# Convolution diagonals built on chip, and W1 loads issued two pairs ahead

## The chip, the cores and the metric

One Trainium2 chip, all 8 cores, each with two of the 16 sequences. The time is that of one launch, in device microseconds of the slowest core. TensorE, VectorE, ScalarE and GpSimd compute; SyncE (SP) and GpSimd (POOL) issue the DMAs.

## The reference, cut to what matters

A pre-norm transformer layer on x of [16, 2048, 1024]: attention with 16 heads, then a feed-forward part with quantised weights and activations.

```python
def bit_linear(x, w):   # activations to int8 steps per row, weights to -1, 0, 1
    xq = x + stop_gradient(act_quant(x) - x)
    wq = w + stop_gradient(weight_quant(w) - w)
    return einsum('bsd,hd->bsh', xq, wq)
h = bit_linear(x, w1)                      # 1024 -> 4096
h = depthwise_conv1d(h.transpose(0, 2, 1), conv_w, conv_b)   # 3 taps, each channel by itself
h = silu(h.transpose(0, 2, 1))
return bit_linear(h, w2)                   # 4096 -> 1024
```

## The kernel before

Each core runs the same program. It first prepares the weights: it casts those of the attention, then (tensor `p_dg`) it builds diagonal matrices for the convolution, and then `wprep` quantises and transposes w1 and w2. These go to HBM: `t_w1t` holds, for each of 32 chunks of 128 hidden channels, 8 blocks of 128x128 bf16 of w1 and 3 diagonal blocks, one for each tap; `t_w2t` holds w2. The diagonal of tap j and chunk hc is the identity times `cw_t`, one VectorE operation per block, 96 in all. Three DMAs from GpSimd write them out, and a barrier of all engines ends the stage.

Then each sequence goes through projections, attention and the feed-forward part. The latter works in `NCT` = 4 blocks of 512 positions (`t`, lines 1191 to 1197). `emit_g1_w1_conv(t)` walks over 16 pairs of chunks (`g`, line 1098). For a pair SyncE issues the load of `w1b`: two chunks of 11 blocks, 704 KB in pieces of 256 bytes, into one of two halves of the buffer. Each chunk is multiplied by 16 matmuls of 257 positions (`w1_chunk`) into the PSUM tile `hps`; VectorE scales the result and writes it to `Hbq` as bf16; three matmuls with the diagonals of the chunk, each on `Hbq` moved by one position, make the convolution in the same PSUM bank (`emit_conv_silu`), and ScalarE writes its silu to `Hb2`. The convolution of a chunk is issued behind the matmuls of the next chunk. A chunk's matmuls wait for the silu of the chunk two before, since they write to its bank.

`emit_mx` keeps the running maximum and minimum of `Hb2` on VectorE, a batch of 4 chunks every second pair. Behind the last pair `emit_chain` makes the scales of the second product out of them: a chain of small steps between VectorE and TensorE. With these scales `emit_hq_batch` rounds `Hb2` to `hqg`, 4 chunks a call.

The second product of block t-1 is issued between the chunks of block t: `emit_w2_sub`, twice a pair, 8 matmuls of 512 columns, with a load of 512 KB of `w2b` (two halves of a buffer, `w2b_cons`). Pairs 0 to 7 make the first 256 positions of the block, pairs 8 to 15 the others. Behind pair 7 and pair 15 `emit_final_pair` evicts two 128-row outputs, one after the other, through the single buffer `obuf`, and the next half product waits for `ve_ev`, the last of these evictions. The second product of the last block runs by itself at the end.

The order on each engine is that in which the calls are written. So on SyncE the loads stand in the order w1 of pair g, w2 of its first half product, w2 of its second. The load of w1 waits for all matmuls issued so far:

```python
if t > 0 or g >= 2:
    r.wait(r.sync, tn, tn.v)
dl_w1[g] = dw1[wb].inc(r.sync.dma_start(...))
r.wait(r.tensor, dw1[wb], dl_w1[g])
```

Nearly every instruction is replayed from one line, so the profile shows line 80 for all; tiles tell them apart.

Of the kernel before, what the change touches and what calls it, by code (L numbers as in the profile page):

```python
# [7 lines left out]
F32 = mybir.dt.float32  # L8
BF16 = mybir.dt.bfloat16
# [82 lines left out]
def build_program(nseq, S):  # L92
# [22 lines left out]
    t_tri = nc.dram_tensor("trimask", [128, 128], BF16, kind="ExternalInput").ap()  # L115
    t_o8 = nc.dram_tensor("ones8s", [8, 128, 8], BF16, kind="ExternalInput").ap()
    t_out = nc.dram_tensor("out", [nseq, S, D], F32, kind="ExternalOutput").ap()
    t_w1t = nc.dram_tensor("w1t_s", [32, 11, 128, 128], BF16, kind="Internal").ap()
    t_wq4 = nc.dram_tensor("wq4_s", [4, 128, 8192], BF16, kind="Internal").ap()
    t_w2t = nc.dram_tensor("w2t_s", [32, 128, D], BF16, kind="Internal").ap()  # L120

# [24 lines left out]
    ctrs = {n: Ctr(nc, es, n) for n in  # L146
            ("bar", "dl", "dw", "dst", "tn", "sc", "ve", "gp",
             "dlx0", "dlx1", "dlx2", "dlx3", "dlb0", "dlb1",
             "dw1a", "dw1b", "dw2a", "dw2b")}
    bar, dl, dw, dst = ctrs["bar"], ctrs["dl"], ctrs["dw"], ctrs["dst"]  # L150
    tn, sc, ve, gp = ctrs["tn"], ctrs["sc"], ctrs["ve"], ctrs["gp"]
    dlx = (ctrs["dlx0"], ctrs["dlx1"], ctrs["dlx2"], ctrs["dlx3"])
    dlb = (ctrs["dlb0"], ctrs["dlb1"])
    dw1 = (ctrs["dw1a"], ctrs["dw1b"])
    dw2 = (ctrs["dw2a"], ctrs["dw2b"])

    r = Rec(nc)
# [45 lines left out]
    with nc.sbuf_tensor("p_wst", [128, 4096], F32) as wstg, \  # L203
         nc.sbuf_tensor("p_wbf", [128, 8192], BF16) as wbf:
        ve_cast = [0, 0]
        dw_w = 0
        for i4, t_w in enumerate((t_qw, t_kw, t_vw, t_ow)):
            if i4 < 3:
                wsrc = t_w.rearrange("h (mc p) d -> mc p h d", p=128)
            else:  # L210
                wsrc = t_ow.rearrange("(hp hh) d m -> hp (hh d) m", hh=2)
            for k4 in range(4):
                par = k4 % 2
                if i4 + k4 > 0:
# [25 lines left out]
        r.wait(r.gpsimd, dw, dw.v)  # L240
        r.emit()
        barrier()
        r.emit()

    with nc.sbuf_tensor("p_dg", [128, 32 * 384], BF16) as dstg:
        ve_dg = 0
        for hc in range(32):
            for j in range(3):
                ve_dg = ve.inc(r.vector.tensor_scalar(
                    dstg[:, hc * 384 + j * 128:hc * 384 + (j + 1) * 128],  # L250
                    ident_f32[:, :],
                    cw_t[:, j * 32 + hc:j * 32 + hc + 1], 0.0,
                    ALU.mult, ALU.add))
        r.wait(r.gpsimd, ve, ve_dg)
        for j in range(3):
            dw.inc(r.gpsimd.dma_start(
                out=t_w1t[:, 8 + j].rearrange("hc p f -> p hc f"),
                in_=dstg.rearrange("p (hc j f) -> p hc j f", hc=32, j=3)
                [:, :, j, :]), 16)
        r.wait(r.gpsimd, dw, dw.v)  # L260
        r.emit()
        barrier()
        r.emit()
# [114 lines left out]
    for s in range(nseq):  # L378
# [389 lines left out]
        if True:  # L768
# [14 lines left out]
            for tq in range(NT // 4):  # L783
# [96 lines left out]
            G1sb = es_c.enter_context(  # L880
                nc.sbuf_tensor(f"c_g1b{s}", [128, 514], F32))
            w1b = es_c.enter_context(
                nc.sbuf_tensor(f"c_w1b{s}", [128, 2 * 2816], BF16))
            w2b = es_c.enter_context(
                nc.sbuf_tensor(f"c_w2b{s}", [128, 2 * 2048], BF16))
            ct1 = es_c.enter_context(
                nc.sbuf_tensor(f"c_t1{s}", [128, 2 * 512], F32))
            ct2 = es_c.enter_context(
                nc.sbuf_tensor(f"c_t2{s}", [128, 2 * 512], F32))
# [13 lines left out]
            sc_sil = [0] * 32  # L903
            ve_hq = [0] * 32
            tn_cv = [0] * 32
            ve_mx = 0
            ve_ev = 0
            ve_g1 = 0
# [66 lines left out]

            def emit_conv_silu(t, hc):
                par = hc % 2
                gpair = hc // 2
                dbase = ((gpair % 2) * 2 + (hc % 2)) * 1408 + 1024
                r.wait(r.tensor, ve, ve_h[hc])  # L980
                for j in range(3):
                    tn.inc(r.tensor.matmul(
                        hps[:, par * 1024:par * 1024 + 512],
                        w1b[:, dbase + j * 128:dbase + (j + 1) * 128],
                        Hbq[:, hc * 514 + j:hc * 514 + j + 512],
                        start=(j == 0), stop=(j == 2)))
                tn_cv[hc] = tn.v
# [44 lines left out]
            def emit_g1_w1_conv(t, w2t=None):  # L1032
# [37 lines left out]
                def w1_chunk(hc, wb):  # L1070
# [5 lines left out]
                    lbase = (wb * 2 + (hc % 2)) * 1408  # L1076
                    for fc in range(8):
                        wsl = w1b[:, lbase + fc * 128:lbase + (fc + 1) * 128]
                        tn.inc(r.tensor.matmul(
# [15 lines left out]
                                [[2048, 128], [512, 2], [1, 257]]),  # L1095
                        G1sb.rearrange("p (b c) -> p b c", b=2)))

                for g in range(16):
                    wb = g % 2
                    if t > 0 or g >= 2:  # L1100
                        r.wait(r.sync, tn, tn.v)
                    dl_w1[g] = dw1[wb].inc(r.sync.dma_start(
                        out=w1b[:, wb * 2816:(wb + 1) * 2816].rearrange(
                            "p (l f h) -> p l f h", l=2, f=11),
                        in_=t_w1t[2 * g:2 * g + 2].rearrange(
                            "l f p h -> p l f h")), 16)
                    r.wait(r.tensor, dw1[wb], dl_w1[g])
                    if g == 0:
                        r.wait(r.tensor, ve, ve_g1)
                    w1_chunk(2 * g, wb)  # L1110
                    if g > 0:
                        emit_conv_silu(t, 2 * g - 1)
                    if w2t is not None:
                        emit_w2_sub(w2t, g // 8, 2 * (g % 8))
                    w1_chunk(2 * g + 1, wb)
                    emit_conv_silu(t, 2 * g)
                    if w2t is not None:
                        emit_w2_sub(w2t, g // 8, 2 * (g % 8) + 1)
# [150 lines left out]
```

How the kernel before makes its waits and increments, by code:

```python
    def inc(self, h, k=1):  # L30
        h.then_inc(self.sem, k)
        self.v += k
        return self.v
# [6 lines left out]
    def then_inc(self, sem, k):  # L40
        self.entry["incs"].append((sem, k))
        return self
# [27 lines left out]
    def wait(self, engrec, ctr, v=None):  # L70
        if v is None:
            v = ctr.v
        assert v <= ctr.v, "wait on future value -> deadlock"
        if v > 0:
            engrec.wait_ge(ctr.sem, v)
# [2 lines left out]
        def replay(ops, eng):  # L78
            for en in ops:
                h = getattr(eng, en["name"])(*en["args"], **en["kwargs"])
                for sem, k in en["incs"]:
                    h.then_inc(sem, k)
# [76 lines left out]
    def barrier():  # L159
        base = bar.v
        for e in ENGS:
            er = getattr(r, e)
            bar.inc(er.nop() if e in ("sync", "gpsimd") else er.drain())
        for e in ENGS:
            getattr(r, e).wait_ge(bar.sem, base + 5)
```

## Time and profile before

| | |
|---|---|
| median of 3 runs | 5727.65 us (5727.33 to 5730.46) |
| profiled execution, its own time | 5722.93 us |
| its span, slowest core | 5721.4 us (the others from 5706.1) |
| TensorE busy | 2964.1 us, 52% |
| VectorE busy | 1648.7 us, 29% |
| ScalarE busy | 1024.0 us, 18% |
| mean granted TensorE clock | 0.756 to 0.759 on the 8 cores |
| HBM read, written | 360.94 MB, 45.09 MB |

The span is from the first to the last instruction of the core; the profiled execution's time lies 1.5 us above it. Busy shares are means over stages that differ a lot: weight preparation, projections, attention, feed-forward. In the rows, c_w1b, c_w2b, c_hp, c_op, c_H, c_mx, c_hq and c_obf are `w1b`, `w2b`, `hps`, `ops`, `Hbq`/`Hb2`, `mxt`, `hqg` and `obuf`; PE, DVE, ACT are TensorE, VectorE, ScalarE; SPq and POOLq issue DMAs.

### The profile page before, as it was taken

The numbers are of one execution on the slowest core, as the hardware profiler recorded it, in microseconds if no ns is written. First come the engines' busy times: TensorE is split into PE (matmuls) and PEld (weight loads), VectorE is DVE, ScalarE is ACT, GpSimd is POOL, SyncE is SP. The second block draws the span as 40 slices with busy tenths as digits, with TensorE's granted clock in tenths as the row PEclk, the third lists the DMA queues.
The fourth block names the chain that finished last, engine by engine and source line by source line (L and its number), as shares of the span: only waits on it lengthen the run. The fifth ranks groups of instructions, "written<-read, shape, count | busy, mean of one in ns | idle before, by whom it ended". The sixth has DMA issues, their size and how long they took to land. (4 is left out here: it accounts for less than half of the span.)

```text
span 5721.4 us, 48041 instructions; the slowest of 8 cores (5706.1 to 5721.4 us)
## 1 busy us (share of the span) xinstructions
PE 2964.1 (52%) x16882; PEld 1512.3 (26%) x17064; DVE 1648.7 (29%) x3867; ACT 1024.0 (18%) x1088; POOL 50.5 (1%) x71
## 2 busy tenths in 40 slices
PE   0010146546777255656565466466674456666564
PEld 0010112213333133333333122133332233333331
DVE  1121322143222613323234111242215323232313
ACT  0122201114455010000000011134461000000000
POOL 0000000000000000000000000000000000000000
PEclk9999999855555577878777798655655677778778
DMA  6464420000000022434343400000000124334344
GB/s 141 154 174 142 162 88 30 15 8 16 16 16 1 8 56 63 119 94 114 90 117 109 159 22 15 22 15 16 16 1 8 40 41 113 100 99 114 91 115 140
DMA packets 567769, 409.15 MB, mean 72 GB/s; under 512 B 438642, under 2 KB 471538, under 8 KB 565492
## 3 DMA queue, kind: packets, MB, share of 16 engines
q1 hardware_dynamic: 555460, 360.97, 22.4%
q0 software_dynamic: 12080, 45.09, 2.4%
q8 instruction: 147, 2.41, 0.2%
q14 instruction: 82, 0.67, 0.0%
HBM read 360.94 MB, written 45.09 MB: 71 GB/s over the span
## 5 line engine op out<-in xcount | busy, mean ns | idle before, releaser
L80 PE MATMUL c_hp<-c_xq,c_w1b 128*128 128x257 bf16 x4096 | 701.6, 344 | 731.7 <-DMA c_w1b<-w1t_s 699.1
L80 PEld LDWEIGHTS c_hp<-c_xq,c_w1b 128*128 128x128 bf16 x4096 | 483.6, 121 | 970.2 <-issue 809.7
L80 ACT ACTIVATE b_pt<-b_lp,b_cb 128x1024 bf16<-128x1024 f32 (+3 forms) x640 | 622.9, 986 | 614.4 <-PE b_lp L80 395.7
L80 DVE TENSOR_TENSOR c_H<-c_hp,c_g1b 128x514 bf16<-128x514 f32 x256 | 177.4, 693 | 1392.1 <-PE c_hp L80 1392.1
L80 PE MATMUL c_op<-c_w2b,c_hq 128*128 128x512 bf16 x2032 | 519.9, 401 | 82.2 <-DMA c_w2b<-w2t_s 58.7
L80 PE MATMUL b_av<-V,b_pt 128*128 128x65 bf16 x5120 | 381.5, 240 | 323.1 <-DVE b_pt L80 224.4
L80 ACT ACTIVATE c_H<-c_hp,c_cb 128x512 bf16<-128x512 f32 x256 | 175.9, 687 | 1984.6 <-PE c_hp L80 1225.3
L80 PEld LDWEIGHTS b_av<-V,b_pt 128*128 128x128 bf16 x5120 | 295.4, 125 | 619.3 <-issue 619.3
L80 PE MATMUL b_lp<-Q,K 64*128 64x512 bf16 x1280 | 373.5, 599 | 11.0 <-DVE x L80 9.3
L80 PEld LDWEIGHTS c_op<-c_w2b,c_hq 128*128 128x128 bf16 x2048 | 210.3, 105 | 388.7 <-issue 201.2
L80 DVE TENSOR_TENSOR b_pt<-b_pt,c_tri 128x128 bf16<-128x128 bf16 x512 | 92.2, 221 | 671.3 <-ACT b_pt L80 671.1
L80 PE MATMUL c_hp<-c_H,c_w1b 128*128 128x512 bf16 x654 | 233.2, 464 | 16.7 <-issue 13.3
L80 PE MATMUL wq_tpw<-c_idb,wq_bw 128*128 128x128 bf16 x512 | 64.7, 306 | 278.5 <-DVE wq_bw L80 233.2
L80 PE MATMUL wp_psw<-c_oc,wp_asw 128*1 128x1 f32 x4 | 0.4, 163 | 393.9 <-DVE wp_asw L80 393.9
L80 PE MATMUL a_vp<-a_vw,a_xh 128*128 128x512 bf16 x496 | 161.6, 482 | 37.4 <-DVE a_xh L80 36.6
L80 ACT ACT_TABLE_LOAD x14 | 18.0, 1283 | 897.6 <-DMA wp_stw<-w 278.5
L80 DVE TENSOR_TENSOR c_t<-c_H,c_ss 128x512 f32<-128x512 bf16 x256 | 165.3, 687 | 18.1 <-issue 8.5
L80 PE MATMUL b_lp<-b_ow,b_tt 128*128 128x512 bf16 x496 | 134.9, 420 | 56.9 <-DVE b_tt L80 56.9
L80 PE MATMUL a_qk<-a_xh,a_kw 128*128 128x512 bf16 x504 | 120.3, 378 | 60.3 <-ACT K L80 52.4
L80 PE MATMUL a_qk<-a_xh,a_qw 128*128 128x512 bf16 x500 | 118.9, 378 | 51.9 <-ACT Q L80 51.6
L80 PE MATMUL c_tp<-c_idb,c_xm 128*128 128x128 bf16 x256 | 32.4, 306 | 212.3 <-DVEq L80 189.6
L80 PE MATMUL b_ut<-b_sq,c_o 128*8 128x512 bf16 x128 | 75.0, 586 | 116.4 <-DVE b_sq L80 116.4
(121 smaller groups left out, 2231.2 us busy)
## 6 DMA issues: line engine op xcount, KB each, us to landing
c_w2b<-w2t_s SPq DMA_DIRECT2D x256, 512.0 KB, 5.3
c_w1b<-w1t_s SPq DMA_DIRECT2D x128, 704.0 KB, 5.2
wp_stw<-w SPq DMA_DIRECT2D x8, 4096.0 KB
wq_stw<-w SPq DMA_DIRECT2D x16, 2048.0 KB, 9.4
a_xt<-x SPq DMA_DIRECT2D x32, 512.0 KB, 3.4
b_xr<-x SPq DMA_DIRECT2D x32, 512.0 KB, 3.3
out<-c_obf POOLq DMA_DIRECT2D x32, 512.0 KB, 3.0
wq_s<-p_wbf POOLq DMA_DIRECT2D x16, 512.0 KB, 7.1
```

Of the source, the lines that this page charges most:

```text
L80: h = getattr(eng, en["name"])(*en["args"], **en["kwargs"])
```

## The change

The diagonals no longer go through HBM. The stage that built all of them is taken out, with its three DMAs and its barrier, and `t_w1t` holds 8 blocks a chunk, so that a load of `w1b` is 512 KB. VectorE builds the three diagonals of a chunk when they are due (`dg_build`), in each of the 4 blocks of each sequence, into one of three slots of `dgb`; a slot is free when the convolution of three chunks before is done. `w1b` has three slots in place of two, a counter for each, and `w1_load(g + 2)` is issued ahead of pair g; it waits for the matmuls of the pair that had the slot (`slot_free`), not for all matmuls issued. `ct2` is cut to the half that is used.

```diff
-    t_w1t = nc.dram_tensor("w1t_s", [32, 11, 128, 128], BF16, kind="Internal").ap()
+    t_w1t = nc.dram_tensor("w1t_s", [32, 8, 128, 128], BF16, kind="Internal").ap()
...
-    dw1 = (ctrs["dw1a"], ctrs["dw1b"])
+    dw1 = (ctrs["dw1a"], ctrs["dw1b"], ctrs["dw1c"])
...
-    with nc.sbuf_tensor("p_dg", [128, 32 * 384], BF16) as dstg:
-        ve_dg = 0
-        for hc in range(32):
-            for j in range(3):
-                ve_dg = ve.inc(r.vector.tensor_scalar(
-                    dstg[:, hc * 384 + j * 128:hc * 384 + (j + 1) * 128],
-                    ident_f32[:, :],
-                    cw_t[:, j * 32 + hc:j * 32 + hc + 1], 0.0,
-                    ALU.mult, ALU.add))
-        r.wait(r.gpsimd, ve, ve_dg)
-        for j in range(3):
-            dw.inc(r.gpsimd.dma_start(
...
                 r.wait(r.tensor, ve, ve_h[hc])
+                r.wait(r.tensor, ve, ve_dgb[hc])
...
-                        w1b[:, dbase + j * 128:dbase + (j + 1) * 128],
+                        dgb[:, dbase + j * 128:dbase + (j + 1) * 128],
...
+                def w1_load(k):
+                    sl = k % 3
+                    r.wait(r.sync, tn, slot_free[sl])
+                    dl_w1[k] = dw1[sl].inc(r.sync.dma_start(
+                        out=w1b[:, sl * 2048:(sl + 1) * 2048].rearrange(
+                            "p (l f h) -> p l f h", l=2, f=8),
+                        in_=t_w1t[2 * k:2 * k + 2].rearrange(
+                            "l f p h -> p l f h")), 16)
+
+                def dg_build(hc):
+                    r.wait(r.vector, tn, tn_cv[(hc - 3) % 32])
+                    for j in range(3):
+                        ve_dgb[hc] = ve.inc(r.vector.tensor_scalar(
+                            dgb[:, (hc % 3) * 384 + j * 128:
+                                (hc % 3) * 384 + (j + 1) * 128],
+                            ident_f32[:, :],
+                            cw_t[:, j * 32 + hc:j * 32 + hc + 1], 0.0,
+                            ALU.mult, ALU.add))
...
+                dg_build(0)
+                w1_load(0)
+                w1_load(1)
                 for g in range(16):
-                    wb = g % 2
-                    if t > 0 or g >= 2:
-                        r.wait(r.sync, tn, tn.v)
-                    dl_w1[g] = dw1[wb].inc(r.sync.dma_start(
...
+                    sl = g % 3
+                    if g + 2 <= 15:
+                        w1_load(g + 2)
+                    dg_build(2 * g + 1)
+                    if g == 0:
+                        dg_build(2)
+                    r.wait(r.tensor, dw1[sl], dl_w1[g])
...
-                    w1_chunk(2 * g, wb)
+                    w1_chunk(2 * g, sl)
                     if g > 0:
                         emit_conv_silu(t, 2 * g - 1)
+                        if g < 15:
+                            dg_build(2 * g + 2)
...
-                    w1_chunk(2 * g + 1, wb)
+                    w1_chunk(2 * g + 1, sl)
+                    slot_free[sl] = tn.v
                     emit_conv_silu(t, 2 * g)
```

## Rows read from the trace of the kernel before

**Rows 1.** The page: busy times of the engines, and the costliest group.

```profile
PE 2964.1 (52%) x16882; PEld 1512.3 (26%) x17064; DVE 1648.7 (29%) x3867; ACT 1024.0 (18%) x1088; POOL 50.5 (1%) x71
...
L80 PE MATMUL c_hp<-c_xq,c_w1b 128*128 128x257 bf16 x4096 | 701.6, 344 | 731.7 <-DMA c_w1b<-w1t_s 699.1
```

**Rows 2.** Block t=0: c_w1b's loads (tile view), then TensorE's timeline.

```profile
L80 SPq DMA_DIRECT2D c_w1b<-w1t_s x14: 359/360/360, 4505.2 to 4682.7; - x14
...
4499.02 1.95 PE L80 MATMUL c_hp<-c_xq,c_w1b 128*128 128x257 bf16 x16 [2.21 <-ACT c_H L80]
...
4502.55 1.94 PE L80 MATMUL c_hp<-c_xq,c_w1b 128*128 128x257 bf16 x16 [0.93 <-ACT c_H L80]
```

**Rows 3.** Timeline of block t=3: start, us, engine, operation, idle time before.

```profile
5380.45 0.36 SPq L80 DMA_DIRECT2D c_w1b<-w1t_s  x1
...
5386.14 3.60 PE L80 MATMUL c_hp<-c_xq,c_w1b 128*128 128x257 bf16 x16 [5.77 <-DMA c_w1b<-w1t_s]
...
5393.11 1.95 PE L80 MATMUL c_hp<-c_xq,c_w1b 128*128 128x257 bf16 x16
...
5394.90 0.81 PE L80 MATMUL c_hp<-c_H,c_w1b 128*128 128x512 bf16 x3
...
5395.55 1.89 PE L80 MATMUL c_op<-c_w2b,c_hq 128*128 128x512 bf16 x8
...
5397.51 0.36 SPq L80 DMA_DIRECT2D c_w1b<-w1t_s  x1
```

**Rows 4.** Windows of blocks 1 to 3, one boundary; last columns: granted clock, DMA share, GB/s.

```profile
2240.40:3090.10 849.70, 524.76 (x2579) 303.12 (x2628) 255.35 (x539) 65.28 (x95) 5.36 (x10) 0.79 0.39 107
...
4721.60:5581.80 860.20, 529.97 (x2580) 304.39 (x2629) 255.37 (x539) 65.28 (x95) 5.33 (x10) 0.78 0.39 106
...
5281.90:5314.00 32.10, 7.93 (x21) 3.16 (x19) 18.29 (x46) 0.69 (x1) 1.07 (x2) 0.57 0.08 33
```

**Rows 5.** Timeline of the diagonal stage, and the next stage's first load.

```profile
175.53 18.89 DVE L80 TENSOR_SCALAR p_dg<-c_idf,c_cw 128x128 bf16<-128x128 f32 x96 [5.68 <-PEq L84]
...
215.73 0.35 SPq L80 DMA_DIRECT2D wp_stw<-w  x1
```

**Rows 6.** The w2 load issued at 5380.9 (tile view); a w1 load alone (windows).

```profile
L80 SPq DMA_DIRECT2D c_w2b<-w2t_s x1: 2337/2337/2337, 5380.9 to 5380.9; - x1
...
DMA to landing us min/median/max: 6.3/6.3/6.3
...
4532.30:4537.60 5.30, 0.00 (x0) 0.00 (x0) 0.07 (x1) 0.69 (x1) 0.00 (x0) 0.77 0.66 136
```

**Rows 7.** VectorE's timeline in block t=3.

```profile
5395.17 0.69 DVE L80 TENSOR_TENSOR c_H<-c_hp,c_g1b 128x514 bf16<-128x514 f32 x1 [4.62 <-PE c_hp L80]
...
5395.78 0.41 DVE L80 TENSOR_TENSOR c_mx<-c_mx,c_H 128x512 bf16<-128x512 bf16 x1
...
5398.97 1.29 DVE L80 TENSOR_TENSOR c_t<-c_H,c_ss 128x512 f32<-128x512 bf16 x2 [0.21 <-issue]
...
5401.30 1.29 DVE L80 TENSOR_TENSOR c_t<-c_H,c_ss 128x512 f32<-128x512 bf16 x2
```

**Rows 8.** Timelines behind pair 7 (t=2), and at a boundary.

```profile
5149.81 1.89 PE L80 MATMUL c_op<-c_w2b,c_hq 128*128 128x512 bf16 x8
...
5153.84 0.53 POOL L80 DMA_DIRECT2D out<-c_obf  x1 [158.18 <-DVEq L80]
...
5159.41 1.41 DVE L80 SCALAR_TENSOR_TENSOR c_obf<-c_op,c_g,x 128x512 f32<-128x512 f32 x2 [6.12 <-PE c_hp L80]
...
5283.98 0.53 POOL L80 DMA_DIRECT2D out<-c_obf  x1 [122.06 <-DVEq L80]
...
5286.97 1.41 DVE L80 SCALAR_TENSOR_TENSOR c_obf<-c_op,c_g,x 128x512 f32<-128x512 f32 x2 [3.55 <-DMA out<-c_obf]
```

**Rows 9.** Windows: projection stage; first chunk of a pair, t=3.

```profile
928.00:952.00 24.00, 15.44 (x65) 5.68 (x64) 0.00 (x0) 6.18 (x10) 0.00 (x0) 1.00 0.00 0
...
5386.10:5389.90 3.80, 3.60 (x16) 2.54 (x18) 0.05 (x1) 0.00 (x0) 0.00 (x0) 0.50 0.41 154
```

More of the change, by code:

```diff
@@ L148, in build_program @@
              "dlx0", "dlx1", "dlx2", "dlx3", "dlb0", "dlb1",
-             "dw1a", "dw1b", "dw2a", "dw2b")}
+             "dw1a", "dw1b", "dw1c", "dw2a", "dw2b")}
     bar, dl, dw, dst = ctrs["bar"], ctrs["dl"], ctrs["dw"], ctrs["dst"]
@@ L239, in build_program @@
                     in_=wbf[:, k4 * 2048:(k4 + 1) * 2048]), 16)
[L240 to L243, printed above, removed]
-    with nc.sbuf_tensor("p_dg", [128, 32 * 384], BF16) as dstg:
-        ve_dg = 0
-        for hc in range(32):
-            for j in range(3):
-                ve_dg = ve.inc(r.vector.tensor_scalar(
-                    dstg[:, hc * 384 + j * 128:hc * 384 + (j + 1) * 128],
-                    ident_f32[:, :],
-                    cw_t[:, j * 32 + hc:j * 32 + hc + 1], 0.0,
-                    ALU.mult, ALU.add))
-        r.wait(r.gpsimd, ve, ve_dg)
-        for j in range(3):
-            dw.inc(r.gpsimd.dma_start(
-                out=t_w1t[:, 8 + j].rearrange("hc p f -> p hc f"),
-                in_=dstg.rearrange("p (hc j f) -> p hc j f", hc=32, j=3)
-                [:, :, j, :]), 16)
         r.wait(r.gpsimd, dw, dw.v)
@@ L882, in build_program @@
             w1b = es_c.enter_context(
-                nc.sbuf_tensor(f"c_w1b{s}", [128, 2 * 2816], BF16))
+                nc.sbuf_tensor(f"c_w1b{s}", [128, 3 * 2048], BF16))
             w2b = es_c.enter_context(
                 nc.sbuf_tensor(f"c_w2b{s}", [128, 2 * 2048], BF16))
+            dgb = es_c.enter_context(
+                nc.sbuf_tensor(f"c_dg{s}", [128, 3 * 384], BF16))
             ct1 = es_c.enter_context(
@@ L888, in build_program @@
             ct2 = es_c.enter_context(
-                nc.sbuf_tensor(f"c_t2{s}", [128, 2 * 512], F32))
+                nc.sbuf_tensor(f"c_t2{s}", [128, 512], F32))
             mxt = es_c.enter_context(
@@ L905, in build_program @@
             tn_cv = [0] * 32
+            ve_dgb = [0] * 32
+            slot_free = [0, 0, 0]
             ve_mx = 0
@@ L977, in emit_conv_silu @@
                 par = hc % 2
-                gpair = hc // 2
-                dbase = ((gpair % 2) * 2 + (hc % 2)) * 1408 + 1024
+                dbase = (hc % 3) * 384
                 r.wait(r.tensor, ve, ve_h[hc])
+                r.wait(r.tensor, ve, ve_dgb[hc])
                 for j in range(3):
@@ L1068, in emit_g1_w1_conv, with w1_chunk @@
                 ve_g1 = ve.inc(r.vector.drain())
-                def w1_chunk(hc, wb):
+                def w1_load(k):
[15 more added lines that the diff above has]
+                            ALU.mult, ALU.add))
+                def w1_chunk(hc, sl):
                     par = hc % 2
@@ L1075, in w1_chunk @@
                         r.wait(r.tensor, ve, st_ch[t - 1])
-                    lbase = (wb * 2 + (hc % 2)) * 1408
+                    lbase = sl * 2048 + (hc % 2) * 1024
                     for fc in range(8):
@@ L1096, in w1_chunk @@
                         G1sb.rearrange("p (b c) -> p b c", b=2)))
+                dg_build(0)
+                w1_load(0)
+                w1_load(1)
                 for g in range(16):
-                    wb = g % 2
-                    if t > 0 or g >= 2:
-                        r.wait(r.sync, tn, tn.v)
-                    dl_w1[g] = dw1[wb].inc(r.sync.dma_start(
[L1103 to L1107, printed above, removed]
+                    sl = g % 3
[5 more added lines that the diff above has]
+                    r.wait(r.tensor, dw1[sl], dl_w1[g])
                     if g == 0:
                         r.wait(r.tensor, ve, ve_g1)
-                    w1_chunk(2 * g, wb)
+                    w1_chunk(2 * g, sl)
                     if g > 0:
                         emit_conv_silu(t, 2 * g - 1)
+                        if g < 15:
+                            dg_build(2 * g + 2)
                     if w2t is not None:
                         emit_w2_sub(w2t, g // 8, 2 * (g % 8))
-                    w1_chunk(2 * g + 1, wb)
+                    w1_chunk(2 * g + 1, sl)
+                    slot_free[sl] = tn.v
                     emit_conv_silu(t, 2 * g)
```

## The prediction

> **What bounds the kernel now.** I began with the page's busy times. TensorE has 2964 us of the span and no engine has more, so none is full; the widest single hole is named in its costliest group: the first matrix product waited 699 us for its weights' load [rows 1]. VectorE, which gets new work here, is busy 1649 us. The waits and the timeline then show where the 699 us sit. In the first position block of a sequence (t=0) a pair of hidden chunks takes 13.65 us: its fourteen loads go out from 4505.2 to 4682.7, thirteen distances [rows 2]. In the other three blocks (t = 1 to 3, which also carry the second product of block t-1) the load is issued at 5380.45, only when the last matmul of the pair before is done, TensorE stands still for 5.77 us, and the next load goes out at 5397.51, 17.06 us later [rows 3]. The wait costs twice: the 16 matmuls behind it take 3.60 us, the same 16 in the second chunk 1.95 us. I read that as the clock: behind the idle stretch 0.50 was granted, the level of 1.2 GHz [rows 9], and the second chunk runs almost twice as fast, at 2.4 GHz. So 5.8 + 1.7 us of 17 go to the late load.
>
> I next measured the six blocks with a second product, from the first load to the last matmul of that product. The two windows hold 849.7 and 860.2 us, each with two boundaries of 32.1 us between blocks [rows 4]. What remains is 785.5 + 796.0 = 1581.5 us for 96 pairs, 16.5 us each.
>
> **The sum, part by part.** It is made against the profiled execution's own 5722.9 us; the median of the runs is 4.7 us above that.
>
> *The diagonal stage before the weight preparation* goes. It begins at 175.53 and the next stage's first load is issued at 215.73; nothing runs beside it [rows 5]. Gain 40.2 us.
>
> *Block t=0.* With the loads two pairs ahead, TensorE waits only for ScalarE. Without a load wait one chunk starts 3.53 us after the last (4499.02 to 4502.55), 0.93 us of it idle [rows 2], so a pair takes 7.06 us. Fourteen pairs in each of two sequences: 28 x (13.65 - 7.06) = 184.6 us. The first two pairs have their loads early already. VectorE's extra work (below, 1.2 us a pair) lies beside the matmuls; with its cover gone it would cost 38 us over 32 pairs.
>
> *Blocks t = 1 to 3, TensorE alone.* At the high clock a chunk's matmuls take 1.79 us (5393.11 to 5394.90), a convolution 0.65 us (to 5395.55), half of the second product 1.73 us: its 1.89 less the 0.16 by which a busy time outlasts the distance of starts (1.95 against 1.79) [rows 3]. Two of each: 8.34 us a pair. Sixteen pairs, less one convolution that the first lacks: 132.8 us. The first chunk of a block begins 0.9 us behind the old load's issue (the copy of the broadcast scales, 514 elements like the multiply of [rows 7]: 0.69 and 0.2 to hand over), and it still meets a cold clock: 3.60 - 1.95 = 1.7 us.
>
> *The wait that takes the old one's place.* On SyncE the load for pair g+2 waits for the end of chunk 2g-1, and the load for half product 2g is queued behind it. From there TensorE has 0.65 + 1.73 + 1.79 + 0.65 = 4.82 us until that half product. Now the w2 load is issued 0.45 us after the w1 load and lands 6.3 us later, 6.75 in all [rows 6]. The w1 load shrinks from 704 to 512 KB: alone it kept the DMA engines 0.66 x 5.3 = 3.5 us, so 3/11 of that, 0.95 us, goes. Landing at 5.80, it is late by d = 1.0 us in each pair. Bounds: 0, if it no longer queues behind the larger load, and 6.75 - 4.82 = 1.93, if nothing is won. I take 1.0. The second half product's load waits for the half product two before, has 6.6 us, and is hidden.
>
> *VectorE.* A diagonal operation costs 18.89 / 96 = 0.197 us [rows 5], six a pair, 1.2 us; I take it unchanged though it now shares the engine (its upper bound by the nearest row is a 0.61 us multiply, for four times as many elements). In every two pairs of 0 to 6 it has twelve of these, four multiplies (0.61), one maximum batch (3.19, to the first rounding) and two rounding batches of 2 x 2.33 [rows 7]: 17.3 us against TensorE's 16.7 us. So in pairs 0 to 6 VectorE is as full as TensorE. Its batches delay the half product behind them: after an even pair 0.27 + 0.61 + 3.19 + 2.33 = 6.40 us pass before the values are ready, where TensorE comes after 4.82. That is 1.6 us late in pairs 3, 5 and 7, in which it covers d. Pairs 1 to 7 then cost 4 x 1.0 + 3 x 1.6 = 8.8 us, pairs 9 to 15 another 7.0. The waits of the diagonals on the convolution three chunks before are met by then; behind them stand the multiplies, which have a chunk of slack.
>
> *Behind pair 7* the first half's outputs leave through one buffer. The half product ended at 5151.70, the output DMA went out at 5153.84, and only at 5159.41 did the second pair of evictions start; they end at 5160.8, 9.1 us after, since each pair takes 1.41 us [rows 8]. The next half product needs them, and TensorE is there after 2.44 us. Before, the load's wait hid this. It leaves 6.7 us; where the second evictions follow the DMA's issue in 3.0 us, as at a boundary (5283.98 to 5286.97), and not in 5.6, it is 4.1 [rows 8]. I take 5.4 us, and 1.7 us for a cold clock afterwards: 7.1 us.
>
> A block: 132.8 + 0.9 + 1.7 + 8.8 + 7.0 + 7.1 = 158.3 us; six of them 949.8. Gain 1581.5 - 949.8 = 631.7 us. Boundaries stay as they are: their chain of small VectorE steps doesn't change, and the final half-only product of the last block doesn't either.
>
> Sum: 40.2 + 184.6 + 631.7 = 856.5 us; 5722.9 - 856.5 = 4866, and beside the median about 4870 us.
>
> **Rivals.** *Nothing new is exposed but VectorE.* d = 0, output landing quick: a block costs 132.8 + 0.9 + 1.7 + 4.8 + 5.8 = 146.0, in all 4793 us. For it: it takes only a w2 load that lands in 4.4 us; against it: behind w1's it took 6.3 [rows 6].
>
> *The half product's load stays as late as now* (d = 1.93, quick landing not met): 132.8 + 0.9 + 1.7 + 27.0 + 8.4 = 170.8 a block, 4941 us. It is the upper end of my own case.
>
> *The clock doesn't stay high.* In the six blocks it was granted 0.78 to 0.79 on average [rows 4]. If a fuller TensorE gets some 0.8 throughout, a block's matmuls take 132.8 / 0.8 = 166 us. The load is then in time, and with 0.9, 5.4 and 1.2 for the rest a block is 173.5 us. At t=0 a half pair grows by 0.61 us, 56 times. Gain 731 us, 4992 us. Against it: the projection stage, 64% busy, was granted 1.00 over 24 us [rows 9]. The Trainium skill, "TensorE: Matmul & The Clock Gate", Part 1, has a rule of this kind: three cores of a die in dense matmuls are held at 13/16 of the clock. The trace of before, in its projection stage, does not show it.
>
> *Block t=0 stays cold*, since its 0.93 us holes return in every chunk: a half pair is 3.44 + 1.30 + 1.09 = 5.8 us, and 28 pairs save 57 us in place of 185: 4994 us. Against it: the chunks at 4499 and 4502 had such holes and took 1.95 us [rows 2].
>
> *Slower after all: the wait moves to the half product in full.* The w2 load stands behind a load that SyncE may issue only late; were it late enough the prefetch would only trade waits. To eat 856.5 us, each of the 96 pairs must lose 8.9 us more; d would be 9.9, a landing 14.7 us after w1's issue where 6.75 was seen. Only with DMA engines at less than half their present speed.
>
> **How the numbers follow.** My case, 4800 to 4941: 0.58. Only VectorE exposed: 0.17. Clock about 0.8: 0.11. Cold t=0: 0.07. Something between or two of these: 0.05. No gain or a loss: 0.02. The range 4780 to 5000 takes in the bounds of d and of the output wait, the d = 0 case and the two clock cases. A measurement of this kernel tells 0.2%, some 11 us, from no change; faster by more than that 0.98, within it 0.01, slower 0.01.
>
> **What would show it.** Right: no wait of the first product on its load but for a sequence's first; a pair at t=0 in 7.1 us, later pairs in 8.3 to 10 us, all chunks behind a block's first in 1.95 us; short waits of the second product on its load in nearly every pair; one hole of 4 to 7 us at pair 8. The sum fails if the second product's wait is near 0 or above 2 us, if chunks of 2.2 us or more stand in the middle of a block, if VectorE's batches slow by sharing, or if the boundaries grow.

## The result, and the profile after

The changed kernel takes 5019.8 us (median of 9 runs, 4990.2 to 5041.8) beside 5727.5 us for the kernel before (10 runs): ratio 0.8763, 95% interval 0.8743 to 0.8783. The direction was right and the size was not: I had forecast 4870 us, in a range up to 5000. The profiled execution took 5002.3 us (span 5000.7), so 720.6 us came off where 856.5 were summed. The 136 us between them are what this study is about. The median lies 17.5 us above that execution, where 4.7 us had been taken over from the kernel before: the time is that of the slowest core, and the eight cores' spans now run from 4947.0 to 5000.7 us, where they ran from 5706.1 to 5721.4.

The page of the changed kernel, busy times and the two groups of the feed-forward matmuls (busy us, mean ns of one | idle time before them and what ended it), and behind it the second product's group on the page of before:

```profile
PE 2751.4 (55%) x16882; PEld 1415.8 (28%) x17064; DVE 1783.6 (36%) x4539; ACT 1023.1 (20%) x1088; POOL 45.5 (1%) x68
...
L80 PE MATMUL c_op<-c_w2b,c_hq 128*128 128x512 bf16 x2032 | 525.0, 404 | 275.7 <-DMA c_w2b<-w2t_s 201.1
L80 PE MATMUL c_hp<-c_xq,c_w1b 128*128 128x257 bf16 x4096 | 528.6, 285 | 67.2 <-ACT c_H L80 58.3
```

```profile
L80 PE MATMUL c_op<-c_w2b,c_hq 128*128 128x512 bf16 x2032 | 519.9, 401 | 82.2 <-DMA c_w2b<-w2t_s 58.7
```

The 699 us for which the first product waited for its load [rows 1] are gone (no idle time before it is put down to that load any more), and its matmuls take 285 ns in place of 344. But the second product now waits 201 us for its own load. Before it waited 59 us, all of that in the two tails, in which the last block's second product runs by itself. Of the 201 us 61 lie in the tails and 140 in the six blocks.

Block t=0, TensorE's timeline; it answers to [rows 2]:

```profile
4182.03 1.94 PE L80 MATMUL c_hp<-c_xq,c_w1b 128*128 128x257 bf16 x16 [0.93 <-ACT c_H L80]
4183.81 0.81 PE L80 MATMUL c_hp<-c_H,c_dg 128*128 128x512 bf16 x3
4185.55 1.95 PE L80 MATMUL c_hp<-c_xq,c_w1b 128*128 128x257 bf16 x16 [0.93 <-ACT c_H L80]
```

A chunk every 3.52 us with 0.93 us idle: the forecast 3.53.

Block t=2, TensorE's timeline (start, us, operation, idle time before); it answers to [rows 3]:

```profile
4479.20 1.89 PE L80 MATMUL c_op<-c_w2b,c_hq 128*128 128x512 bf16 x8 [1.62 <-DMA c_w2b<-w2t_s]
...
4490.13 3.56 PE L80 MATMUL c_op<-c_w2b,c_hq 128*128 128x512 bf16 x8 [2.45 <-DMA c_w2b<-w2t_s]
...
4501.71 1.89 PE L80 MATMUL c_op<-c_w2b,c_hq 128*128 128x512 bf16 x8 [1.41 <-DMA c_w2b<-w2t_s]
...
4571.10 2.63 PE L80 MATMUL c_op<-c_w2b,c_hq 128*128 128x512 bf16 x8 [2.95 <-DMA c_w2b<-w2t_s]
...
4573.53 2.91 PE L80 MATMUL c_hp<-c_xq,c_w1b 128*128 128x257 bf16 x16
...
4608.29 1.89 PE L80 MATMUL c_op<-c_w2b,c_hq 128*128 128x512 bf16 x8 [2.89 <-DMA c_w2b<-w2t_s]
```

The reader sees the wait that I had called d, once a pair. It was to be 1.0 us. The eleven in this block are of 1.38 to 2.97 us: four of the first five between 1.4 and 1.7, the later ones between 2.25 and 2.97. In the six blocks there are 66 of over a microsecond, 2.1 us each on average, the longest 3.67. And what follows a wait of over two microseconds can be slow, as it was behind four of the seven such waits: the same eight matmuls take 1.89, 3.56 or 2.63 us, a chunk 1.95 or 2.91. The windows of those stretches (length, busy times, granted clock, DMA share, GB/s):

```profile
4487.70:4490.10 2.40, 0.00 (x0) 0.00 (x1) 2.19 (x9) 0.69 (x1) 0.00 (x0) 1.00 0.74 275
4490.10:4493.50 3.40, 3.37 (x9) 1.17 (x10) 0.08 (x1) 0.00 (x0) 0.00 (x0) 0.51 0.02 9
4565.50:4568.10 2.60, 2.55 (x20) 1.77 (x18) 2.27 (x8) 0.00 (x0) 0.00 (x0) 1.00 1.01 242
4571.10:4573.50 2.40, 2.40 (x8) 0.94 (x9) 0.00 (x0) 0.00 (x0) 0.00 (x0) 0.71 0.11 42
4573.50:4576.20 2.70, 2.70 (x17) 2.01 (x16) 0.00 (x0) 0.00 (x0) 0.00 (x0) 0.63 0.00 0
```

Dense work is granted 1.00; in the row behind 2.4 us with no matmul it is 0.51, the level of 1.2 GHz, and 0.63 to 0.71 in rows that lie between the two levels. So a wait for the second product's load can cost more than its own length, as the old one did: of its 41 waits of 2.0 us and more in this trace 21 were followed by slow matmuls, of the 80 shorter ones (0.4 us and more) none.

Why is the load late? SyncE's timeline of that last pair, and the tile view of its first w2 load (issue to landing in the last line), which answer to [rows 6]:

```profile
4563.42 0.36 SPq L80 DMA_DIRECT2D c_w1b<-w1t_s  x1
...
4563.87 2.28 SPq L80 DMA_DIRECT2D c_w2b<-w2t_s  x2
```

```profile
L80 SPq DMA_DIRECT2D c_w2b<-w2t_s x1: 1321/1321/1321, 4563.9 to 4563.9; - x1
...
DMA to landing us min/median/max: 7.1/7.1/7.1
```

The distance that TensorE leaves is as forecast: from 4563.42 it is ready at 4568.15, 4.73 us later (4.82 in the sum). The load is not: it lands 7.1 us after its issue, 7.6 behind the w1 load's. At 4495.56 it was 6.1 behind (the wait ended at 4501.71). I had summed 5.80 (6.75 less 0.95). Over the six blocks a pair's first w2 load lands 5.2 to 7.8 us after its issue, median 6.4; in the kernel before it was 6.0 to 7.8, median 6.3. The w1 load ahead of it lands after 4.3 us in place of 5.3.

The other places named ahead, the hole behind pair 7 and the boundary behind pair 15 (TensorE, POOL's queue, VectorE), answer to [rows 8]:

```profile
4557.60 3.57 PE L80 MATMUL c_op<-c_w2b,c_hq 128*128 128x512 bf16 x8 [5.89 <-DVEq L80]
...
4560.97 2.27 PE L80 MATMUL c_hp<-c_xq,c_w1b 128*128 128x257 bf16 x15
```

```profile
4431.15 0.53 POOL L80 DMA_DIRECT2D out<-c_obf  x1 [88.06 <-DVEq L80]
...
4436.90 1.41 DVE L80 SCALAR_TENSOR_TENSOR c_obf<-c_op,c_g,x 128x512 f32<-128x512 f32 x2 [6.30 <-DMA out<-c_obf]
...
4438.86 0.53 POOL L80 DMA_DIRECT2D out<-c_obf  x1 [7.18 <-DVEq L80]
```

The hole is there, 5.9 us and a cold half product after it. At the boundary the second evictions now begin 5.75 us behind the first output's DMA, where it was 3.0. Around that output three w1 loads and two w2 loads of the next block are on their way, issued from 4.4 us ahead of it to 2.4 us behind it; before there was none.

**The ledger.** Measured as in the prediction, the six blocks with a second product take 173.1, 176.7, 176.0, 180.1, 179.2 and 182.7 us, together 1067.9 where 949.8 were forecast: 118 of the 136 us. The four inner boundaries take 35.2 us where before they took 32.1: 12 us. The stage gives 30.2 and not 40.2 us (from the span's start to the next stage's first load): 10 us. That is 140; the start of the feed-forward part came some 5 us earlier than the stage explains, and the rest of the parts agree within 1 or 2 us.

### The profile page after: what moved, and what is told of

Its sections match the earlier page's. It is cut to its first block and busy times, and to the rows that moved or that the text cites. A ratio compares the mean times of both kernels' runs of the same rounds, so it can differ in the third digit from the quotient of the medians.

```text
span 5000.7 us, 49180 instructions; the slowest of 8 cores (4947.0 to 5000.7 us)
## 1 busy us (share of the span) xinstructions
PE 2751.4 (55%) x16882; PEld 1415.8 (28%) x17064; DVE 1783.6 (36%) x4539; ACT 1023.1 (20%) x1088; POOL 45.5 (1%) x68
## 5 line engine op out<-in xcount | busy, mean ns | idle before, releaser
L80 PE MATMUL c_hp<-c_xq,c_w1b 128*128 128x257 bf16 x4096 | 528.6, 285 | 67.2 <-ACT c_H L80 58.3
L80 PEld LDWEIGHTS c_hp<-c_xq,c_w1b 128*128 128x128 bf16 x4096 | 413.2, 102 | 210.6 <-issue 110.2
L80 PEld LDWEIGHTS c_op<-c_w2b,c_hq 128*128 128x128 bf16 x2048 | 199.4, 102 | 574.5 <-issue 384.7
L80 DVE TENSOR_TENSOR c_H<-c_hp,c_g1b 128x514 bf16<-128x514 f32 x256 | 176.7, 690 | 519.5 <-PE c_hp L80 519.4
L80 PE MATMUL c_hp<-c_H,c_dg 128*128 128x512 bf16 x654 | 183.0, 379 | 8.1 <-DVE c_dg L80 1.3
L80 DVE TENSOR_SCALAR c_dg<-c_idf,c_cw 128x128 bf16<-128x128 f32 x768 | 171.5, 281 | 21.0 <-PE c_hp L80 9.9
```

What stands on the lines that cost most here:

```text
L80: h = getattr(eng, en["name"])(*en["args"], **en["kwargs"])
```

## The experiments

### Which load goes first

If the w2 load is late since it stands behind the prefetched w1, it must be enough to issue w1 behind both w2 loads of the pair. Nothing else changes.

```diff
-                    if g + 2 <= 15:
-                        w1_load(g + 2)
                     dg_build(2 * g + 1)
...
                             w2_done[w2t] = tn.v
+                    if g + 2 <= 15:
+                        w1_load(g + 2)
```

> The load of w1 for pair g+2 is issued behind both loads of the second product of pair g, not ahead of them; nothing else changes. In the changed kernel the second product waited 1.4 to 3.0 us in nearly every pair for its first load, which had been issued 0.45 us behind the w1 load and landed 5.5 to 7.1 us later; waits of 2.5 us and more were followed by 2.5 to 3 us of matmuls at the low clock. Theory A (place in the queue): the first w2 load now goes out when its half of the buffer is free, 1.8 us earlier, and no w1 load stands just ahead of it, so the waits fall under 0.5 us and the low clock in mid-block goes: 6 blocks x 14 pairs x about 2.2 us is 185 us, about 4840 us against 5020. Rival B (rate: eight cores now draw at once and each load is slower whatever its place): waits above 1.2 us stay, above 4930 us. Rival C (VectorE is what holds the pairs, the load wait only hides it): waits on the load go and waits on VectorE take their place, above 4950 us.

4848.3 us (4 runs), ratio 0.8458 (0.8444 to 0.8471): 172 us less than the change. Its groups of lines:

```profile
L80 PE MATMUL c_hp<-c_xq,c_w1b 128*128 128x257 bf16 x4096 | 514.0, 280 | 67.2 <-ACT c_H L80 58.3 <-DVEq L80 8.9
L80 PE MATMUL c_op<-c_w2b,c_hq 128*128 128x512 bf16 x2048 | 503.1, 390 | 148.2 <-DVEq L80 84.3 <-DMA c_w2b<-w2t_s 56.7 <-DVE c_dg L80 7.1
```

The wait for w2 is down from 201 to 57 us, all but 0.4 of it in the tails, and so the blocks' 140 us went. With 37 us less of busy time in the two groups (1053.6 to 1017.1), and less 18 us by which the second product's waits for VectorE in the blocks grew (51 to 69), that makes 159 us, beside 163 in the six blocks (1067.9 to 904.9). SyncE's timeline shows how the loads now lie:

```profile
4379.60 0.42 SPq L80 DMA_DIRECT2D c_w1b<-w1t_s  x1
4383.31 4.52 SPq L80 DMA_DIRECT2D c_w2b<-w2t_s  x2
4387.92 0.92 SPq L80 DMA_DIRECT2D c_w1b<-w1t_s  x1
```

They are spread over the pair in place of three within 2.4 us. In the blocks w2's land after 3.4 to 6.7 us (median 4.3, where it was 5.8), w1's after 5.3 to 7.2, where two pairs of slack hide it. The edit does two things at once, and this run does not part them: a pair's first w2 load lands sooner (4.6 us for 6.4), and it goes out sooner, 6.4 us ahead of the point where TensorE is ready for it and not 4.3 (medians).

### Another slot for w2

The other cure gives w2 a third slot, its load issued one half product ahead; w1 goes back to two slots, one pair ahead, so that the space is the same.

```diff
-                nc.sbuf_tensor(f"c_w1b{s}", [128, 3 * 2048], BF16))
+                nc.sbuf_tensor(f"c_w1b{s}", [128, 2 * 2048], BF16))
...
-                nc.sbuf_tensor(f"c_w2b{s}", [128, 2 * 2048], BF16))
+                nc.sbuf_tensor(f"c_w2b{s}", [128, 3 * 2048], BF16))
...
-                wb2 = glob % 2
                 g2c = 2 * glob
-                r.wait(r.sync, tn, w2b_cons[wb2])
-                dlw = dw2[wb2].inc(r.sync.dma_start(
...
+                if not w2q:
+                    w2_load()
+                if w2n[0] < 128:
+                    w2_load()
+                wb2, dlw = w2q.pop(0)
...
-                w1_load(1)
...
-                    sl = g % 3
-                    if g + 2 <= 15:
-                        w1_load(g + 2)
+                    sl = g % 2
+                    if g + 1 <= 15:
+                        w1_load(g + 1)
```

> Three slots for the loads of the second product, each issued one half product ahead; the w1 buffer gives up its third slot for that (two slots, the load issued one pair ahead, at the same moment as before). The w1 load still stands ahead of a w2 load in the queue, but each w2 load has at least 8 us. Theory A and B: no wait for w2 inside the blocks, no low clock but at the start of a block and behind the output wait; about 4830 us, and VectorE's waits of about 1.5 us in pairs 3, 5, 7 are what is left. Rival B also sees w1 loads late now and then. Rival C: above 4950 us.

4797.3 us, ratio 0.8374 (0.8358 to 0.8390). Its group of lines, and TensorE in the middle of a block:

```profile
L80 PE MATMUL c_op<-c_w2b,c_hq 128*128 128x512 bf16 x2048 | 503.4, 392 | 109.1 <-DVEq L80 81.6 <-DMA c_w2b<-w2t_s 20.0 <-DVE c_dg L80 5.5
```

```profile
4343.19 1.95 PE L80 MATMUL c_hp<-c_xq,c_w1b 128*128 128x257 bf16 x16
4344.98 0.81 PE L80 MATMUL c_hp<-c_H,c_dg 128*128 128x512 bf16 x3
4345.62 1.89 PE L80 MATMUL c_op<-c_w2b,c_hq 128*128 128x512 bf16 x8
4347.35 1.95 PE L80 MATMUL c_hp<-c_xq,c_w1b 128*128 128x257 bf16 x16
...
4351.51 1.95 PE L80 MATMUL c_hp<-c_xq,c_w1b 128*128 128x257 bf16 x16
```

From 4343.19 to 4351.51, 8.32 us: the pair of the sum (8.34), met once no load is late. The blocks take 149.4 to 150.4 us, within a microsecond or two of those with the order changed (150.3 to 152.2). Here the loads still land slowly (median of all w2 loads 5.5 us); they are only asked for sooner, and that alone is enough. So two cures of one suspected wait give the same block, and the wait is the cause. The rest of the 51 us between the two lies elsewhere: two tails of 131 us (to the last output) become 113.5 and 116, since their waits for w2 shrink from 56 to 20 us, and the boundaries 33.6 to 34.6 in place of 37 to 38.

### Larger pieces

Is the lateness one of DMA time? Here w1 lies in HBM by partition, so that its load is made of pieces of 2 KB in place of 256 bytes; order and slots are those of the change.

```diff
-    t_w1t = nc.dram_tensor("w1t_s", [32, 8, 128, 128], BF16, kind="Internal").ap()
+    t_w1t = nc.dram_tensor("w1t_s", [32, 128, 1024], BF16, kind="Internal").ap()
...
-                            "l f p h -> p l f h")), 16)
+                            "l p x -> p l x")), 16)
```

> The scratch copy of w1 is laid out so that a load moves pieces of 2 KB in place of 256 bytes; places in the queue stay those of the changed kernel. Theory: the w1 load then keeps the DMA engines about as long as a w2 load of the same size, some 1.6 us in place of 2.5, so the w2 load behind it lands about 1 us sooner, the waits of 1.4 to 3.0 us become 0.5 to 2 us and the low clock behind them mostly goes: 4890 to 4930 us. Rival (the load is late by fixed latency or by memory shared with other cores, not by w1's many small pieces): no more than 20 us, near 5000 us.

4888.6 us, ratio 0.8534 (0.8514 to 0.8553): 131 us less. The page's DMA issues, of the change and then of this kernel (last number: median us from issue to landing):

```profile
c_w2b<-w2t_s SPq DMA_DIRECT2D x256, 512.0 KB, 5.4
c_w1b<-w1t_s SPq DMA_DIRECT2D x128, 512.0 KB, 4.4
```

```profile
c_w2b<-w2t_s SPq DMA_DIRECT2D x256, 512.0 KB, 4.5
c_w1b<-w1t_s SPq DMA_DIRECT2D x128, 512.0 KB, 3.9
```

The same bytes in larger pieces land 0.5 us sooner, and the w2 loads 0.9 us sooner, those right behind w1 even 1.5 (median 4.9 for 6.4); the wait for w2 falls to 100 us in all, blocks to 156 to 160 us. The piece size of one load moves the landing of the next, here by more than its own. The Trainium skill, "DMA: Bandwidth & Descriptors", "Why small descriptors are slow (HBM only)", has a fixed cost for each packet, 3 cycles of 11 at 256 bytes; the trace agrees in direction, and 0.5 of 4.4 us is less than that share, latency included.

### The diagonals alone, and the prefetch alone

One kernel has the diagonals built by VectorE and 512 KB loads, but two slots and the old wait for all matmuls; the other has the prefetch, but a stage that builds the diagonals once, writes them by one DMA in larger pieces, and loads 192 KB of them for each pair. First the edit of the one, then of the other:

```diff
-                    sl = k % 3
-                    r.wait(r.sync, tn, slot_free[sl])
+                    sl = k % 2
+                    if t > 0 or k >= 2:
+                        r.wait(r.sync, tn, tn.v)
...
-                w1_load(0)
-                w1_load(1)
                 for g in range(16):
-                    sl = g % 3
-                    if g + 2 <= 15:
-                        w1_load(g + 2)
+                    sl = g % 2
+                    w1_load(g)
```

```diff
+        dw.inc(r.gpsimd.dma_start(
+            out=t_dgs.rearrange("k p x -> p k x"),
+            in_=dstg.rearrange("p (k x) -> p k x", k=16)), 16)
...
-                def dg_build(hc):
...
+                def dg_load(k):
+                    sl = k % 2
+                    r.wait(r.sync, tn, tn_cv[(2 * k - 3) % 32])
+                    ve_dgb[k] = ddg[sl].inc(r.sync.dma_start(
+                        out=dgb[:, sl * 768:(sl + 1) * 768],
+                        in_=t_dgs[k]), 16)
```

> One part of the change alone: diagonals built by VectorE, loads of 512 KB, but two slots and the load issued only behind all matmuls of the pair before, as in the old kernel. Theory: the diagonal stage's 40 us go, each of about 126 waits is about 0.9 us shorter, VectorE's work is hidden behind the waits: 150 to 160 us less than before, near 5570 us. Rival (building costs what VectorE spends, 151 us): near 5700 us.

> The prefetch alone: the stage that builds the diagonals and writes them to HBM is back (its rows are 1.5 KB here), the diagonals of a pair come by a load of 192 KB of their own, issued one pair ahead, and VectorE builds none in the blocks. Theory: 40 us come back with the stage; the extra load stands ahead of the second w2 load, which has room; the first w2 load's waits stay: 5050 to 5080 us. Rival (VectorE's building costs the blocks time): 5020 us or less.

Diagonals alone: 5590.7 us, ratio 0.9754 (0.9736 to 0.9773), 137 us less than before, where 150 to 160 were expected. Its group of lines:

```profile
L80 PE MATMUL c_hp<-c_xq,c_w1b 128*128 128x257 bf16 x4096 | 704.8, 345 | 602.9 <-DMA c_w1b<-w1t_s 570.6 <-ACT c_H L80 32.3
```

The wait is 128 us shorter over 126 loads, 1.0 us for each 192 KB less (0.95 in the sum), and the matmuls are as cold as before. This trace also shows the step of the sum by itself, since here only the w1 load shrank and kept its place: w1 lands after 4.2 to 4.3 us on every core, 1.0 sooner, but the w2 load 0.45 us behind it after 6.0 to 6.2, where it was 6.3 (medians). Prefetch alone: 5007.7 us, ratio 0.8743 (0.8727 to 0.8759), no different from the whole change as far as the two intervals tell, and under the 5050 to 5080 expected. The rival had named such a time, but for VectorE's sake, which the next section tries. w2 is waited for as long:

```profile
L80 PE MATMUL c_op<-c_w2b,c_hq 128*128 128x512 bf16 x2032 | 519.3, 401 | 275.3 <-DMA c_w2b<-w2t_s 195.3 <-DVEq L80 65.6 <-DVE c_t L80 10.0
```

So the gain is the prefetch's; the two parts do not add up, since both shorten the same wait for w1. In this kernel the second w2 load of a pair is issued 4.8 us behind the first, in place of 1.9, and the first still lands after 5.8 to 6.0 us (medians of the cores; 5.8 to 6.4 in the changed kernel). It is late without a third load close behind it.

### The stage, where loads aren't late

That the stage came back at no price was odd, but the blocks of these kernels scatter by 10 us and more. I repeated it on the version with three w2 slots, whose blocks repeat within 1 us, and, on the same base, let GpSimd build the diagonals. The edit for the stage is the one above; that for GpSimd:

```diff
-                    r.wait(r.vector, tn, tn_cv[(hc - 3) % 32])
+                    r.wait(r.gpsimd, tn, dg_user[hc % 3])
...
-                        ve_dgb[hc] = ve.inc(r.vector.tensor_scalar(
+                        ve_dgb[hc] = gp.inc(r.gpsimd.tensor_scalar(
```

> On top of the three w2 slots (4797 us): GpSimd builds the diagonals, not VectorE. The waits of the second product on VectorE's batches (about 1.5 us in pairs 3, 5, 7) come from the chain multiply, maximum batch, rounding batch, in which no diagonal stands. Theory: at most 10 us, 4785 to 4797 us. Rival (VectorE is full in pairs 0 to 6, each 1.2 us a pair that it is spared is gained): 7 pairs x 1.2 us x 6 blocks is 50 us, 4745 us. A third case: GpSimd is slow at it or disturbs VectorE, above 4830 us.

> Version with three slots for the second product's weights, but with the diagonals built once in a stage of their own, written to HBM and loaded for each pair of chunks (192 KB a pair). It sizes the diagonal stage where the weights' loads aren't late: the same version with VectorE building them took 4797 us. Theory A (the stage's 40 us are real, building in the blocks costs nothing): 4797 + 40 = 4837 us, plus whatever the 192 KB loads cost. Theory B (what the stage cost is returned as VectorE's time in the blocks, 6 operations of 0.2 us a pair beside batches that TensorE waits for): 4797 +- 10 us, and blocks that are shorter than 150 us by some 7 us each.

GpSimd: 4813.6 us, ratio 0.8408 (0.8387 to 0.8429), blocks of 149.0 to 149.6. Diagonals from HBM: 4815.7 us, ratio 0.8402 (0.8391 to 0.8414), blocks of 147.7 to 149.8. Building them on VectorE: 4797.3 and 149.4 to 150.4. Taking 768 operations off VectorE shortens a block by about 1 us; so in these blocks TensorE hardly waits for them. In all GpSimd wins nothing with it: the kernel is 16 us slower, where a gain of up to 10 had been expected; the trace has these in many small places outside the blocks. One operation takes it 544 ns, VectorE 281.

```profile
L80 POOL TENSOR_SCALAR c_dg<-c_idf,c_cw 128x128 bf16<-128x128 f32 x768 | 406.5, 544 | 3274.7 <-PEq L80 2525.0 <-PE c_hp L80 741.4 <-PE c_op L80 8.0
```

With the stage in place the kernel is 18 us slower, between the two theories. SyncE's timeline, of the kernel with the stage and then of the changed one: the last load of the attention weights ahead of it, and the first of the stage behind it.

```profile
125.94 29.72 SPq L80 DMA_DIRECT2D p_wst<-ow  x4
206.42 66.00 SPq L80 DMA_DIRECT2D wp_stw<-w  x4
```

```profile
137.26 29.37 SPq L80 DMA_DIRECT2D p_wst<-ow  x4
185.54 66.02 SPq L80 DMA_DIRECT2D wp_stw<-w  x4
```

From the one load to the other is 80.5 us with this stage and 48.3 without, so 32 us (88.4 and 40.1 with the stage of before, which writes smaller pieces: that is the 40.2 of the sum). But ahead of it the loads of the attention weights run 11 us slower without it. On all eight cores of eleven kernels the load of 'ow' goes out at 119 to 129 us in the three kernels that have the stage, and at 129 to 144 in the eight without. I can't say why; the instructions ahead of that load are the same. It eats 10 of the 40 us that I had summed, and 11 of the 32 here; the 21 left are near the 18 measured.

### One core alone

Do the other seven cores' loads make mine late? The changed kernel on one core (the other cores' outputs are copies of its own).

```diff
-    for i in range(ncores):
+    for i in range(1):
...
-    res = run_bass_kernel_spmd(nc, in_maps, core_ids=list(range(ncores)))
+    res = run_bass_kernel_spmd(nc, in_maps, core_ids=[0])
```

> The changed kernel on one core alone, with the two sequences of the first core; the rest of the output is filled with copies of them. The question is why the first w2 load lands 5.5 to 7.1 us after its issue where I had forecast 5.35. If the memory shared with the other cores is the cause, it lands within 5.3 us here, the waits of the second product fall under 1 us and the span is about 4850 us. If the cause lies in the core's own queue and DMA engines (behind the w1 load and beside the second w2 load), landings and waits stay as on eight cores, span about 4970 us.

4898.5 us, a single run, between the two times that were expected:

```profile
L80 PE MATMUL c_op<-c_w2b,c_hq 128*128 128x512 bf16 x2048 | 515.8, 398 | 245.0 <-DMA c_w2b<-w2t_s 182.9 <-DVEq L80 58.7 <-DVE c_t L80 3.4
```

183 of the 201 us of waits stay. In the blocks they are 125 us, and on the eight cores of the changed kernel they are 119 to 144; a pair's first w2 load lands after 5.9 us (5.2 to 7.5), and there after 5.8 to 6.4 (medians). So the late load is in the main the core's own doing, in its own queue; the neighbours add at most some tenths of a microsecond to each. They cost time elsewhere: of the 104 us by which this span is shorter 35 lie ahead of the load of 'ow', which goes out at 102.6 us and not at 137.3, and 48 in the six blocks, whose sum, 1013 us, is that of the fastest of the eight cores (1014 to 1062).

### A second output buffer, and all together

The hole behind pair 7 was forecast at 5.4 + 1.7 us. On the version with three w2 slots the second output goes through `ct1`, the scratch of the rounding, which is idle then, with its own counter (the rounding waits for that output's DMA); then the larger pieces are added.

```diff
-                    r.wait(r.vector, dst, gp_ob)
+                    ob = obuf if vv == 0 else ct1
+                    r.wait(r.vector, dso[vv], gp_ob[vv])
...
-                    gp_ob = dst.inc(r.gpsimd.dma_start(
+                    gp_ob[vv] = dso[vv].inc(r.gpsimd.dma_start(
```

> On top of the three w2 slots (4797 us): the second output of each final pair is evicted into another buffer (ct1, idle at that time), so that VectorE doesn't wait for the first output's DMA. Theory: the hole behind pair 7 shrinks from 4 to 6 us to about 0.5 us with the low clock behind it, some 6 us in each of 6 blocks, and the same wait at the boundaries, 4 to 5 us in each of 6, goes too: 60 to 70 us, about 4730 us. Rival (the waits are covered by VectorE's other work): above 4780 us.

> Three slots for the second product's weights, a second output buffer, and w1 laid out in pieces of 2 KB. Without the last it took 4715 us. Theory (the load of w1 is no longer waited for, so a quicker one wins nothing inside the blocks; at the boundaries and at block starts it competes less with the outputs): 4700 to 4715 us, blocks 142 us, boundaries 28 to 29. Rival: the second product's loads of [rows 6] still end the wait somewhere, then blocks below 140 us and under 4695 us.

4715.4 us, ratio 0.8231 (0.8217 to 0.8246), 82 us less than without it. POOL's queue shows the two outputs of a block's first half 1.7 us apart, where in the changed kernel they are 6.4 apart:

```profile
4362.44 0.53 POOL L80 DMA_DIRECT2D out<-c_obf  x1 [101.09 <-DVEq L80]
4364.13 0.53 POOL L80 DMA_DIRECT2D out<-c_t  x1 [1.15 <-DVE c_dg L80]
```

Blocks take 142.0 to 143.6 us (7.1 less each, 42 in all, beside 5.4 + 1.7 us in the sum: a hole of 5.9 us and its cold matmuls go, and a wait of 1.2 us for VectorE's batch is left there), boundaries 29.1 to 29.4 (5 less each, 20), and the tails 103 in place of 115 (23): 85. The larger pieces add nothing on top (4716.3 us, ratio 0.8231, 0.8220 to 0.8242): where no load is waited for, a quicker one is worth nothing.

## Why the prediction was right and wrong

- *What bounds it, t=0, TensorE's own time:* right. A chunk at t=0 takes 3.52 us (3.53), a pair that waits for nothing 8.32 (8.34). From its first chunk to the first load or chunk of t=1, block t=0 shrank by 91.5 us in the second sequence (92.3).
- *The wait that takes the old one's place:* the mechanism, the place and TensorE's 4.82 us were right. **The step that failed is d = 1.0 us.** It rests on "the w1 load shrinks ... so 3/11 of that, 0.95 us, goes": I let the w2 load inherit that gain. Measured, w1 did land 1.0 us sooner, but the w2 load behind it took as long as before, 6.4 us against 6.3 (medians), and where the w1 load alone had shrunk it gained 0.1 to 0.3. So d was 2.1 us on average, and beyond my upper bound of 1.93 in 38 of the 66 waits. The bound took one landing, 6.3 us, for all; they went up to 7.8, in the kernel before too.
- *What that step cost:* eleven waits of 1.0 us in each of six blocks are 66 us of the sum; there were 140, 74 more. And the sum has no cold clock behind d, though it had seen that "the wait costs twice": none of the waits under 2.0 us brings it, half of the longer ones do. Slow matmuls took another 37 us. Together 111 of the 118 us of the blocks, but not by themselves: the holes behind pair 7 took 7 us more than summed and VectorE's batches 17 less, and 17 us of smaller items are left, the half product behind a block's first chunk among them, slow as well.
- *"The second half product's load is hidden":* so it is. It is issued 1.9 us behind the first and lands 6.5 us later in the pair shown, and in that pair the engines moved 203 GB/s from 4563.9 to 4571.0, where it was 261 GB/s at the same place before (5381.0 to 5387.2). As the kernel with the prefetch alone shows, it isn't what keeps the first one late.
- *VectorE:* right that its batches hold the second product in pairs 3, 5 and 7. With the loads in time these waits are 1.0, 1.6 and 1.6 us, 4.2 a block (forecast 4.8), with the order changed as with three w2 slots. They were to cover d, 1.6 us against 1.0; with d at 2.1 it is mostly d that covers them, and in the changed kernel only 2.0 us a block are left. With the order changed a block takes 150.3 us and not the 147.3 of the sum with d = 0, since its hole behind pair 7 is 7.3 us and not 5.4. Right that the diagonals cost next to nothing, 1 us a block. One takes 281 ns beside other work, or 0.22 us of busy time (171.5 us over 768), where 0.197 was taken.
- *Behind pair 7:* right, 5.7 to 7.3 us and each time a cold half product. The average, 6.5, is near the upper bound, 6.7, and not at the 5.4 taken.
- *Boundaries:* "stay as they are" was wrong by 3 us each. The next block's first loads are now on their way while the first output is being written, and the second evictions wait for that output. The second buffer, which takes this wait away, brings them to 29. The Trainium skill, "DMA: Bandwidth & Descriptors", "Issuing engines are not separate DMA queues", says that DMAs of all issuing engines run on the same 16 DMA engines and interleave; the 5.75 us in place of 3.0 agree.
- *The stage:* it was worth the 40.2 us, and 10 of them went to slower loads ahead of it.
- *Rivals:* "stays as late as now" (4941) was the nearest, and right in its waits: it gave a block 27.0 us of them, and 25.4 were measured (23.4 for w2, 2.0 for VectorE). What it too left out are the cold clock behind them, 37 us, the boundaries, 12, and the stage's 10: 5000. "Clock at 0.8" is out: in the kernel with two output buffers 40 us in the middle of a block, in which TensorE was busy throughout, are granted 1.00 (below, the slowest core), and so they are on three other cores as busy. Cold t=0 is out. "Only VectorE exposed" (4793) is what the version with three w2 slots reaches, 4797, but not by its parts: its blocks take 150.0 us and not 146.0, and its tails are shorter.

```profile
4380.00:4420.00 40.00, 40.00 (x258) 25.04 (x257) 19.54 (x58) 6.88 (x10) 0.00 (x0) 1.00 0.71 199
```

Open: why the w2 load gains so little from 192 KB less ahead of it (a pair's three loads are all there 8.0 us after the first issue, with 1728 KB before and with 1536 KB now), and why the loads ahead of the diagonal stage run 10 us slower without it.

## What to carry to other kernels

When a load is prefetched on the queue that also carries a load with little slack, issue the one with little slack first: the prefetch alone won 723 us here, and a change of its place in the queue 172 over the whole change. A shorter load ahead does not make the one behind it land sooner by as much: take the whole spread of its landings for the bounds, and ask for each wait of over two microseconds what a cold clock adds. The time is the slowest core's, so a wait that scatters from core to core costs its upper end. When one wait of a pair is removed, look at everything that used to lie beside it: the single output buffer's wait behind pair 7 lay beside that of the load before, and cost 42 us in the blocks after.

## What I had not expected of the hardware

- A 512 KB load that stands behind another 512 KB in pieces of 256 bytes, with a third close behind, lands after 5.2 to 7.8 us (median 6.4); spread over the pair, in the other order, w2 loads land after 3.4 to 6.7 (median 4.3). One core alone shows 5.2 to 7.5 (median 5.9), so little of this is contention between cores. With the load ahead in pieces of 2 KB it is 4.9.
- The clock can fall behind shorter gaps than I had thought, and not behind each: 0.51 was granted behind one of 2.45 us, while behind one of 2.89 us eight matmuls still took 1.89 us.
- GpSimd takes 544 ns for a 128x128 multiply by a column, VectorE 281.
